# Two cross layers of a graph network, their dense products taken by seven block products in place of eight, and the neighbour weight applied ahead of the adjacency

## The reference, cut to what matters

```
z = layernorm(x2)
h = z
for l in (0, 1):
    agg  = segment_sum(h[src], dst, 1250)
    mean = agg * deg_inv[:, None]
    h_new = h @ W_self[l] + mean @ W_neigh[l] + b[l]
    h = relu(h_new) if l == 0 else h_new
y = x2 + h
```

## Time and profile before

| | us |
|---|---|
| three runs | 1470.53, 1471.95, 1473.56 |
| median | 1471.95 |
| span of the profiled execution | 1469.8 |
| PE busy in it | 1409.7 (96%) |
| DVE / ACT / POOL busy | 892.5 / 545.3 / 358.6 |

### The profile page before, as it was taken

The page is one execution under the profiler, slowest core; times in us unless marked ns, Lnnn a source line. Parts: engine busy times, 40 slices in busy tenths (PEclk is TensorE's granted clock), DMA queues, the critical chain, the costliest instruction groups (busy, mean ns, idle before and its releaser), DMA issues.

```text
span 1469.8 us, 28270 instructions
## 1 busy us (share of the span) xinstructions
PE 1409.7 (96%) x8327; PEld 723.4 (49%) x8327; DVE 892.5 (61%) x2053; ACT 545.3 (37%) x758; POOL 358.6 (24%) x373
## 2 busy tenths in 40 slices
PE   6889999999999999999999999999999979999996
PEld 5334454545444444444654444446444435566653
DVE  7988888686988887541542222323357775676652
ACT  4678747373524543220111220001111125565551
POOL 4331230202201210000875003700012311442232
PEclk9999999999999999999999999999999988999998
DMA  7332010000266665543323444430056646889863
GB/s 287 55 76 56 4 58 0 29 0 29 75 197 177 163 170 173 160 127 115 127 74 100 104 98 144 157 126 0 0 173 186 186 179 195 242 247 282 267 166 58
DMA packets 156675, 185.96 MB, mean 127 GB/s; under 512 B 106172, under 2 KB 107659, under 8 KB 156600
## 3 DMA queue, kind: packets, MB, share of 16 engines
q1 hardware_dynamic: 144440, 143.07, 32.0%
q0 software_dynamic: 12160, 41.95, 11.0%
HBM read 118.40 MB, written 41.94 MB: 109 GB/s over the span
## 4 chain that ended last, share of the span: by engine, by line
PE 74%; DVE 12%; issue 6%; ACT 3%; DMA 2%; DVEq 2%; POOL 1%; ACTq 0%; SPq 0%; POOLq 0%
PE ps L1361 30%; PE ps L1432 12%; PE ps L1596 7%; PE ps L1616 6%; PE ps L1261 3%; PE ps L1262 3%; PE ps L1263 3%; PE ps L1192 2%; PE ps L1622 1%; PE ps L1584 1%; ACT th L1700 1%; DVE hm L2085 1%; PE ps L1219 1%; DVE bstat L578 1%; PE ps L1290 1%
## 5 line engine op out<-in xcount | busy, mean ns | idle before, releaser
L1361 PE MATMUL ps<-wa,tb 128*128 128x512 f16 x960 | 208.8, 379 | 0.0
L1432 PE MATMUL ps<-adj,nm 128*128 128x384 f16 (+2 forms) x960 | 169.6, 340 | 0.0
L1261 PE MATMUL ps<-gp,hop 128*128 (+1 forms) x400 | 151.6, 379 | 1.0 <-DVE gn L2159 1.0
L1262 PE MATMUL ps<-gp,hop 128*128 (+1 forms) x400 | 151.6, 379 | 0.0
L1263 PE MATMUL ps<-gp,hop 128*128 (+1 forms) x400 | 151.6, 379 | 0.0
L1361 PEld LDWEIGHTS ps<-wa,tb 128*128 (+1 forms) x960 | 93.3, 98 | 111.4
L1432 PEld LDWEIGHTS ps<-adj,nm 128*128 x960 | 93.9, 98 | 75.4
L1810 ACT ACTIVATE tb<-cx 128x384 f32 (+1 forms) x48 | 26.8, 559 | 273.2 <-DVE cx L2387 273.2
L1361 PE MATMUL ps<-wa,hop 128*128 128x512 f16 x480 | 105.3, 379 | 2.9 <-DVEq L2334 2.9
L1596 PE MATMUL ps<-tkT,wb 128*128 128x314 f16 x768 | 106.0, 301 | 0.8 <-ACT tkT L1883 0.8
L1361 PE MATMUL ps<-wb,hop 128*128 128x512 f16 x480 | 103.8, 379 | 0.0
(11 more groups left out here) (401 smaller groups left out, 2194.8 us busy)
## 6 DMA issues: line engine op xcount, KB each, us to landing
w_st<-in_ew SPq DMA_DIRECT2D x16, 2048.0 KB, 11.7
self_d<-cr SPq DMA_DIRECT2D x20, 512.0 KB, 3.0
cr<-self_d SPq DMA_DIRECT2D x20, 512.0 KB, 3.3
stage<-in_wn POOLq DMA_DIRECT2D x16, 512.0 KB, 3.8
x_d<-cr SPq DMA_DIRECT2D x10, 512.0 KB, 4.7
cx<-x_d SPq DMA_DIRECT2D x10, 512.0 KB, 4.0
cr<-x_d SPq DMA_DIRECT2D x10, 512.0 KB, 4.0
out<-cr SPq DMA_DIRECT2D x10, 512.0 KB, 3.4
```

Source lines behind the costliest of these rows:

```text
L1261: pe.matmul(acc, wh, gh, start=(s_ == 0), stop=False, skip_group_check=True)
L1262: pe.matmul(acc, wh, gl, start=False, stop=False, skip_group_check=True)
L1361: ins = pe.matmul(ps[:, b + c, :], lhs(part, k), w[:, w_, k, c * 512:(c + 1) * 512], start=(k == 0 and part == 0 and w_ == 0), stop=(last ...
L1432: ins = pe.matmul(ps[:, 6 + j, 0:n], nm[:, part, s_, bass.ds(f * P, P)], adj[:, s_, t0 * TP:t0 * TP + n], start=first, stop=(s_ == NT - 1 ...
```

## The change

**The products.** `own0`, `own`, `neighbours` and `row_degrees` go. The rows are now taken in PAIRS_N = 5 pairs of tiles, and a pair's 256x1024 block times the 1024x1024 weight is cut into quarters a11, a12, a21, a22 and b11, b12, b21, b22. Seven products of quarters, of sums of row quarters (s1 to s4) and of sums of weight quarters (t1 to t4) are combined in PSUM and in SBUF, where the plain way has eight:

```
+PRODUCTS = (("a11", "b11"), ("s1", "t1"), ("a22", "t4"), ("s2", "t2"), ("a12", "b21"), ("s4", "b22"), ("s3", "t3"))
+PAIRS_N = 5
+PASSES = 4
...
+            def product(n, right):
+                left = LEFT_OF[right]
+                pe.wait_ge(s_t[left], T_0[left] + 16 * (n + 1))
+                blk, acc = sets[PLACE[n // PAIRS_N]][right], ps[:, bank_of(n, right), :]
+                begins = right in ("b11", "t1", "b21")
+                for k in range(4):
+                    for part, w_ in ((0, 0), (0, 1), (1, 0)):
+                        ins = pe.matmul(acc, slot(n, left)[:, 4 * part + k, :], part_of(blk, w_)[:, k, :],
...
+            def pair(n):
+                if n % PAIRS_N == 0:
+                    pe.wait_ge(s_wd, HALF_ROUNDS * (n // PAIRS_N + 1))
...
+                product(n, "b11")
...
+                product(n, "t1")
+                if n and n - 1 not in LAST_OF_LAYER:
+                    evicted(pe, n - 1, "t3")
+                    product(n - 1, "t4")
+                evicted(pe, n, "b11")
+                product(n, "t2")
...
+                product(n, "b21")
+                evicted(pe, n, "t1")
+                product(n, "b22")
+                evicted(pe, n, "t2")
+                product(n, "t3")
```

**The left sides.** SP loads a pair from DRAM (`load_pair`), turns seven blocks with DMA transposes (`turn_part`) and stores an own pass by quarters (`store_self`). ACT normalises (`normal`) and makes the high parts (`high_a`, `high_s`), DVE takes the statistics, forms the sums of the rows (`sums`) and makes the low parts:

```
+            def low_a_p(m, j):
...
+                    v.tensor_tensor(stg[:, 0:2, 1, :], ys[m % 2][0:TP, 0, :].rearrange("p (b n) -> p b n", b=2),
+                                    stg[:, 0:2, 0, :], ALU.subtract).then_inc(s_lo, 1)
...
+            def sums(m):
...
+                link(v.tensor_tensor(y_[:, 1, right_], y_[:, 1, left], y_[:, 1, right_], ALU.add))
+                v.tensor_tensor(y_[:, 1, left], y_[:, 0, left], y_[:, 1, left], ALU.subtract).then_inc(s_sum, 1)
+                link(v.tensor_tensor(y_[:, 0, left], y_[:, 1, right_], y_[:, 0, left], ALU.subtract))
+                v.tensor_tensor(y_[:, 0, right_], y_[:, 0, right_], y_[:, 0, left], ALU.subtract).then_inc(s_sum, 1)
```

```
+            def lows_of_blocks(k, r, buf):
+                u, c, st = r % 2, r // 2, quads(buf, r % 2)
+                g.wait_ge(s_wh, HALF_ROUNDS * k + r + 1)
+                for right, row, o in (("b11", 0, 0), ("b21", 1, 0), ("b22", 1, 1)):
+                    g.tensor_tensor(piece(k, right, 1, c, u), st[:, row, o], piece(k, right, 0, c, u), ALU.subtract)
+                link(g.tensor_tensor(st[:, 0, 0], st[:, 0, 1], st[:, 0, 0], ALU.subtract))
+                g.tensor_tensor(st[:, 0, 1], st[:, 1, 1], st[:, 0, 1], ALU.subtract)
+                link(g.tensor_tensor(st[:, 1, 1], st[:, 1, 1], st[:, 0, 0], ALU.subtract))
+                g.tensor_tensor(st[:, 1, 0], st[:, 1, 0], st[:, 1, 1], ALU.subtract).then_inc(s_wt, 1)
...
+            def weights_in_pair(k, c):
+                if 1 <= c < 4:
+                    load_weights(k, 2 * c + 1, stage)
+                if c < 4:
+                    lows_of_blocks(k, 2 * c, stage)
+                    if c < 3:
+                        load_weights(k, 2 * c + 2, stage)
+                    lows_of_blocks(k, 2 * c + 1, stage)
```

The weight of a neighbour pass is prepared during the own pass before it (k = 1 and 3), W_self of layer 1 (k = 2) during the adjacency products of layer 0, and W_self of layer 0 (k = 0) during B, where POOL also makes the low parts of the sums (`lows_of_sums`), so that a half round there is eleven operations of 128x256 on POOL. DVE's stream for a pair:

```
+            def pair(n, k, c):
...
+                if stats:
+                    stats_p(n + 2)
+                if own:
+                    evict(n, "b11")
+                if prep:
+                    low_a_p(m, 0), low_a_p(m, 1), sums(m)
+                if own:
+                    if c:
+                        weight_low(k, c - 1, 1)
+                    evict(n, "t1")
+                if stats:
+                    coefficients_p(n + 2)
+                if n and own_pass(n - 1):
+                    evict(n - 1, "t4")
...
+                if prep:
+                    low_s_p(m, 1)
+                if own:
+                    evict(n, "t2")
+                if prep:
+                    low_s_p(m, 0)
+                evict(n, "b21"), evict(n, "b22")
+                if own and c < 4:
+                    weight_low(k, c, 0)
...
+                evict(n, "t3")
```

More of the change, by code:

```diff
@@ L168, in chained @@
         early()
-    with loop(1, NT // 2 - 1, per) as r:
-        at(r, 0), at(r, 1)
+    for r in range(1, NT // 2 - 1):
+        at(r, 0)
+        if then and r == 1:
+            then()
+        at(r, 1)
     at(NT // 2 - 1, 0)
@@ L852, in low_d @@
                 ln_low(g, D_, i, j, cy, dyh[:, j, 0, :], dyh[:, j, 1, :])
-            with g.Fori(0, NT // 2 - 1) as r:
-                for j in range(2):
-                    full_d(r, j), low_d(r, j)
+            add_rest(0), add_rest(1)
+            for t in range(NT - 2):
+                full_d(t // 2, t % 2), low_d(t // 2, t % 2), add_rest(t + 2)
             full_d(NT // 2 - 1, 0), low_d(NT // 2 - 1, 0)
```

825 lines of the change are left out of this document (538 added, 287 removed).

## The result

The changed kernel takes 1567.49 us (median of four runs, 1558.19 to 1573.69) where the kernel before took 1472.28 in the same comparison: a ratio of 1.064 with a 95% interval of 1.0596 to 1.0684. The forecast was 1550 with a range of 1486 to 1594. So the direction and about the size were right: +95 us against +78. Five of its terms were off by 5 to 11 us each, one of them the other way, and one of its mechanisms was the wrong one, so part of the closeness is luck.

A forecast was written before the change was run, and what follows sets the result against it. PE alone was taken to set the time in the cross layers, DVE's chain in stage D. Terms of -33, -1, +30, +14, +30, +23, +7 and +8 made +78 on 1471.95: 1550 us, range 1486 to 1594.

The forecast's parts named there:

- rival C: Own passes and adjacency of layer 0: transfers are late too, adding 33 us to the forecast, 1583 us; chance 0.12.
- PE's own work, minus 33: Five stages up to the start of D: fewer matmuls cut PE's work from 480.1 to 447 us, minus 33.
- B, plus 8: Stage B: more ACT and POOL work for the first weight makes its slots slip; plus 8 us, bounds 0 and 20.
- Own of layer 0, +44 by the sum: Own pass of layer 0: plus 30 for weight preparation and plus 14 for the first pair's wait and statistics.
- weight ring: Own passes: load, POOL, ACT and DVE hand over in turn for each half round; 25.7 us a pair against PE's 18.17.
- Meetings: DVE and POOL exclude each other on SBUF operands; nine tenths of 7.25 us counted per own pair with weight work.
- Own of layer 1, plus 30 by the weight ring: Own pass of layer 1: four pairs with weight work take 25.7 us instead of 18.2, plus 30 us.
- Neighbour passes, nothing: Neighbour passes: no weight work, DVE's 12 or 13 us fit under PE's 18.2 a pair; no cost.
- Adjacency of layer 0, plus 23: Adjacency of layer 0: weight hand-overs of 11.4 us a tile against PE's 8.65, and pair 10's row blocks; plus 23 us.
- D, plus 7: Stage D: a POOL addition of 2.13 us a tile meets DVE's small operations; plus 7 us, between -4 and +13.
- A: Cross layers: the feeding work stays covered and PE remains the bound, so the kernel is faster, 1440 us; chance 0.11.
- B: Own passes: DVE and POOL do not meet, weight preparation takes 19.2 us a pair; 1498 us in all, chance 0.16.

The follow-up runs named there:

- e9: Changed kernel, orders alone: a12's transpose earlier, adjacency of layer 0 reordered, pair 10 prepared at tiles 4 and 5, statistics behind evictions; 1531.10 us, ratio 1.0406.
- e11: Changed kernel, transposes from pair 2, most POOL work for the last three weights and most of D's addition left out, adjacency and statistics reordered; 1472.55 us.
- e3: Changed kernel with six of seven POOL operations of each half round left out for the two weights of layer 1; 1564.03 us.
- e1: Changed kernel with the row-block transposes from pair 2 on replaced by copies of 16 columns; 1547.60 us.
- e10: Changed kernel with the edits of e1 and e3 together, and all but 8 columns of POOL's addition in D left out; 1515.34 us.
- e4: Changed kernel, adjacency of layer 0 reordered: ACT's half rounds one tile later, DVE evicts ahead of the weight, pair 10 prepared at tiles 6 and 7; 1545.18 us.
- e12: e9 with stage D's addition of x2 on DVE, ahead of its wait for PE, instead of on POOL; 1535.40 us, ratio 1.0435.
- e2: Changed kernel with most weight loads from the second weight on cut to 16 of 256 columns; 1541.22 us.
- e7: Changed kernel with the transpose of block a12 issued ahead of s1, s2 and the pair loads; 1559.42 us.

## Why the forecast was right, and which steps were not

The measured 1567 lies 17 us over the forecast's 1550 and 16 under rival C's 1583, and errors of both signs went into that: the size was good, the mechanism of the own passes was not.

- **PE's own work, minus 33: right.** Neighbour passes of 90.6 and, once unloaded, own passes of 90 and an adjacency of 89 are the sum's numbers. PE busy did not fall by 53 us, as the last part of the forecast had it, but by 12, since products behind waits run at a lower granted clock (up to 5.3 us instead of 2.75 for one): that sign was misread, the work was not.
- **`row_degrees`, minus 1:** -3.4 by the starts of B, and -0.3 in the second trace; the term is too small for these runs to tell.
- **B, plus 8:** +7.4. The range of it was 0 to 20. That the slipping of ACT's slots does it was not tried by itself.
- **Own of layer 0, +44 by the sum:** 140.8 and 135.3 us where the forecast had 132.2 (88.2 and 44). The size was right. Of its parts, the first pair's wait was 8.1 us (9.9 in the second trace) for 8.5. The rest was put to a weight ring of 25.7 us and 5 us of statistics; pairs took 29.2, 32.2, 33.8, 25.9 and 19.7. e9 shows that the statistics' place in DVE's order, with a12's transpose moved as well, was worth 8 to 14 us, about the 14 that the forecast gave to first wait and statistics together. e11 shows that 26 us stay when both chains are light, 10 of them PE's slower products, for which the forecast had no term. Meetings cost DVE some 10 us here (96.5 us busy, and 86.7 in e11 with POOL light).
- **Own of layer 1, plus 30 by the weight ring: the failed step.** It came out 5 to 9 us smaller (+24.5, +20.8), and that it came so near is luck. The ring of 25.7 us a pair was not what held the pass: with six of seven POOL operations gone it stayed (e3). The forecast had no term for transposes, stores and landings in an own pass and kept slow ones as a rival, C, that adds to the ring. The runs show them as a second chain beside the ring: transposes out of `stg`, quarter stores and loads with the DMA engines 87% busy. Nor is the ring alone worth 30. Without the transposes the pass takes 101.9, 13.7 over PE's own (e1), although the meetings there are as large as forecast: DVE is busy 80.7 us for 67.6 in e10 and POOL 61.4 for the estimated 47, some 27 us together. The pass lost 13.7 in all, so at least half of these meetings delayed nothing, and adding both engines' meetings to one chain was wrong as well. It needs e1's and e3's edits together to free it (e10).
- **Neighbour passes, nothing:** +6.2 in layer 0 and 0 in layer 1. The sign named for it, a late transpose, is what stands there, once, at the first pair (3.7 us), and e1 took it away.
- **Adjacency of layer 0, plus 23: right mechanism, undersized.** The chain is the one written down, with loads that took 4.7 to 5.2 and 7.4 to 9.6 us in turn to reach ACT instead of the 4.4 counted: 10.8 and 13.6 us a tile, 12.2 in the mean, for 11.4. The larger miss is pair 10's preparation: 6 to 7 forecast, and 17.3 with 5.8 behind it measured, since DVE does it in front of a result that PE waits for. e4 and e9 show that nearly all of it is order (92.9 for PE's own 89.1).
- **D, plus 7:** +12.8 and +11.3. Without the addition D is 8 to 16 us shorter (e10), so the addition is about all of it; the forecast had +13 as its upper end. That it costs by meeting POOL, as forecast, is not shown: on DVE it costs 4 us more (e12).
- **The rules of the Trainium skill.** The Trainium skill, SBUF — State Buffer, "SBUF: two separate sides", calls the port pair that VectorE and GpSimd share an exclusive lock. The trace agrees that one stands while the other runs: after 675.8 us L2650, 128x2 with two SBUF inputs, takes 0.64 us instead of 0.16 and ends with POOL's L950, and L949 ranges from 658 to 1641 ns. The 2.68 us of L2647, which has one tensor input, span several POOL instructions. What failed was not the lock but the sum of its costs into PE's time. The Trainium skill, GPSIMD Engine Reference, "3.1 Elementwise — side-by-side cycle accounting", has about 2.6 cycles an element, an estimated 0.55 us for 128x256. The trace has 0.66 to 0.73, so a short operation has a fixed part besides, as the rows of 80 and 512 columns had said.
- **Rivals.** A (faster) is out: even e11 is not faster. B gave an own pass 4 us, by no meetings; there are meetings, and with no transposes own 1 still loses 13.7 (e1). C named what the forecast lacked, late transfers, and its price, 33 us, is about what e2 took away (22 to 31 us of the whole); but the runs show them beside the ring and not added to it.

No version tried beats the kernel before; the best full one is e9, 4.1% slower.

## What to carry to other kernels

Cutting PE's work by an eighth pays only if what feeds it keeps its distance: here the cut of 33 us brought seven transposes a pair, sums, more half-size copies and two rings of hand-overs, and each had less time than before. Where two engines wait for each other around a loop, look for the second chain as long as the first: taking away one of them shows little or nothing, and only both together tell. And write an in-order engine's stream so that nothing that waits for a transfer stands ahead of what the bound engine waits for: moves of this kind were worth 36 us here with the same work, 29 to 30 of them in the adjacency stage; moving one transpose alone (e7) was worth nothing clear.
